# Two VectorE loops of flow attention written out, with the next tile's scaling ahead of the result

## What is computed

```
def _flow_attention(x, Wq, bq, Wk, bk, Wv, bv, Wo, bo):
    ...
    kv = jnp.einsum('nhld,nhlm->nhdm', k, v * source_competition[..., None])
    o = jnp.einsum('nhld,nhdm->nhlm', q * sink_incoming[..., None], kv)
    o = o * sink_allocation[..., None]
    o = o.transpose(0, 2, 1, 3).reshape(B, L, D)
    return o @ Wo + bo
...
sa = _flow_attention(_layernorm(x, g1, be1), Wq, bq, Wk, bk, Wv, bv, Wo, bo)[0]
x = x + sa
h = _layernorm(x, g2, be2)
h = jax.nn.gelu(h @ W1 + b1, approximate=False) @ W2 + b2
return x + h
```

## Time and profile before

| | us |
|---|---|
| median of 3 runs | 2020.53 |
| lowest and highest run | 2018.15, 2022.69 |
| the profiled execution, its own time | 2014.01 |
| its span, first to last instruction | 2012.2 |
| TensorE busy in the span | 1719.1 |
| VectorE busy | 911.8 |
| ScalarE busy | 535.0 |
| GpSimd busy | 747.8 |

### The profile page before, as it was taken

One profiled execution on the slowest core, in us unless ns is written; L12 is line 12 of the kernel. 1 busy time (PEld: TensorE's weight loads), 2 busy tenths in 40 slices (PEclk: granted clock), 3 DMA queues, 4 the chain that ended last, 5 costly groups with the idle time before them and its releaser, 6 DMA issues. The chain is left out here.

```text
span 2012.2 us, 26298 instructions
## 1 busy us (share of the span) xinstructions
PE 1719.1 (85%) x8051; PEld 1119.1 (56%) x8052; DVE 911.8 (45%) x2251; ACT 535.0 (27%) x1490; POOL 747.8 (37%) x857
## 2 busy tenths in 40 slices
PE   4559988756868888889689999599999999999996
PEld 4124433424447777754344445567776777677763
DVE  5852267343659999979756648300000000000001
ACT  0011111111148888821111115212211222112211
POOL 0577777773048988971011100300000000043007
PEclk9999989988979999999799999699999999999998
DMA  7800021000020000010210012864404400420003
GB/s 226 311 2 2 2 80 33 2 2 1 22 96 0 0 0 0 0 53 0 100 47 0 0 62 107 281 218 187 187 16 188 182 21 16 188 67 21 16 23 105
DMA packets 75240, 144.17 MB, mean 72 GB/s; under 512 B 20825, under 2 KB 22441, under 8 KB 70957
## 3 DMA queue, kind: packets, MB, share of 16 engines
q1 hardware_dynamic: 49201, 119.88, 16.3%
q0 software_dynamic: 18976, 10.95, 2.4%
q10 hardware_dynamic: 7006, 12.69, 1.9%
HBM read 107.75 MB, written 35.69 MB: 71 GB/s over the span
## 5 line engine op out<-in xcount | busy, mean ns | idle before, releaser
L326 POOL DMA_INDIRECT sorted_edges<-fa_records,fa_edge_slot x313 | 313.0, 1000 | 157.9 <-issue 100.4
L1926 PEld LDWEIGHTS et_ps_h<-ex_turned,arena 128*128 128x128 f32 x3072 | 349.3, 193 | 19.6 <-issue 19.6
L1926 PE MATMUL et_ps_h<-ex_turned,arena 128*128 128x128 f32 x3072 | 349.6, 276 | 8.5 <-issue 8.5
L1936 PE MATMUL et_ps_y<-arena,et_hidden_t 128*128 x768 | 337.5, 592 | 0.0
L1844 DVE TENSOR_SCALAR ex_turned<-et_ps_t,ex_ln_g,ex_ln_b 128x128 f32<-128x128 f32 x96 | 32.8, 403 | 580.4 <-PE et_ps_t L1906 580.4
L945 POOL TENSOR_SCALAR ad_row<-iota,ad_edges 128x128 fp32r<-128x128 f32 x295 | 210.6, 726 | 130.7 <-DMA ad_edges<-sorted_edges 101.1
L1936 PEld LDWEIGHTS et_ps_y<-arena,et_hidden_t 128*128 128x128 f32 x768 | 142.2, 190 | 160.7 <-issue 160.7
L994 ACT ACTIVATE ad_row_high<-ad_row,ad_edges 128x128 fp32r<-128x128 f32 x472 | 184.2, 391 | 46.2 <-DVE ad_row L965 33.0
L1016 PE MATMUL ad_ps<-ad_to,ad_row_high 128*128 128x320 f32 x472 | 153.4, 337 | 49.3 <-ACT ad_row_high L994 46.7
L1812 POOL DMA_INDIRECT xn_rows<-slot_out,from_slots x10 | 12.2, 1217 | 476.5 <-POOLq L1809 473.7
L963 DVE TENSOR_SCALAR ad_to<-iota,ad_edges 128x320 fp32r<-128x320 f32 x472 | 167.9, 415 | 20.6 <-DMA ad_edges<-sorted_edges 20.6
(11 more groups left out here) (381 smaller groups left out, 2219.8 us busy)
## 6 DMA issues: line engine op xcount, KB each, us to landing
arena<-L_ffn_W SPq DMA_DIRECT2D x16, 4096.0 KB, 18.5
slot_rows<-fa_zeros SPq DMA_DIRECT2D x1, 7424.0 KB, 26.9
slot_out<-fa_zeros SPq DMA_DIRECT2D x1, 7168.0 KB, 46.2
slot_out<-et_y ACTq DMA_DIRECT2D x24, 256.0 KB, 2.0
et_rows_in<-slot_rows ACTq DMA_DIRECT2D x24, 256.0 KB, 2.7
sorted_edges<-fa_records,fa_edge_slot POOLq DMA_INDIRECT x313, 2.1
arena<-x SPq DMA_DIRECT2D x1, 2500.0 KB
neighbour<-fa_Wv SPq DMA_DIRECT2D x10, 250.0 KB
```

Of the source, the lines that this page charges most:

```text
L326: nc.gpsimd.indirect_dma_start(g.sorted_edges, bass.IndirectOffsetOnAxis(ap=self.edge_slot[0:rows, e:e + 1], axis=0), self.records[0:rows, ...
L1926: last = pe.matmul(ps_h[:, f % 2, i, :], x.weights[:, at:at + P], turned[:, k, :], start=(k == 0), stop=(k == KD - 1))
L1936: last = pe.matmul(ps_y[:], hidden_t[:, i, :], x.weights[:, bass.ds(buffer * (2 * HALF) + (HALF + i * D), D)], start=(i == 0), stop=(i == ...
```

## The change

In both loops VectorE's call of `staggered` is replaced by ten tiles written out. `scale_q(t + 2)` now stands ahead of `attended(t)`, and `prepare_ff(t + 2)` ahead of `add_up(t)`. The orders of the other engines, the semaphores that are waited for and their values per tile, the buffers and the arithmetic are as they were.

```
-            staggered(c, 2, scale_q, attended, nothing)
+            scale_q(0, 0)
+            scale_q(1, 1)
+            for t in range(T):
+                if t + 2 < T:
+                    scale_q(t + 2, t % 2)
+                attended(t, t % 2)
...
-            staggered(c, 8, prepare_ff, nothing, add_up)
+            prepare_ff(0, 0)
+            prepare_ff(1, 1)
+            for t in range(T):
+                if t + 2 < T:
+                    prepare_ff(t + 2, t % 2)
+                add_up(t, t % 2)
```

## The result

The changed kernel took 2009.54 us, the median of four runs (2005.42 to 2010.44), against 2020.67 for the kernel before beside it (2018.15 to 2022.69). That is 11.1 us or 0.55% less by the medians; the ratio of the runs, as it was measured, is 0.9935 with a 95% interval of 0.9914 to 0.9956, which is 13.1 us. The forecast was 2006.0 in a range of 1999.5 to 2013.0, so the time lies in it and on the forecast side, 3.5 us above the value.

The account below looks back on a forecast made before the run. The prediction took the VectorE-TensorE chain through both loops as the bound. Savings of 13.8 us (attention) and 0.7 (feed-forward), 14.5 together, took the median from 2020.53 to 2006.0 us, range 1999.5 to 2013.

Parts of the forecast that it names:

- What bounds it: First block: VectorE and TensorE waiting for each other in turn form one chain through both loops, setting the block's end.
- Part 1: Attention loop: scaling and turn leave the chain, nine periods of 5.24 us, 47.2 against 60.96, 13.8 us less.
- open sizes: Attention loop: product 3.71 or 3.64 us, hand-over to TensorE up to 0.15 or 0.06; 1.1 us of the range.
- The clock's 5.0: Attention loop: three periods stretched by the lower clock return to normal, 5.0 us of the gain if the clock stays up.
- The Trainium skill's pull-ahead of weight loads: Attention loop: product's weight loads could slip under the turn, making 14.4 us instead of 13.8; the last tile spoke against it.
- Part 2: Feed-forward loop: order unchanged, hardware-loop register work goes, 0.12 us a tile over six tiles, 0.7 us less.
- the 14.5: Whole kernel: total predicted saving, 13.8 us from the attention loop plus 0.7 from the feed-forward loop.
- Part 4: After the loops: later stretches and next blocks shift as a whole, GpSimd's scatter stays hidden, block ends near 553.
- The clock did not fall in the attention loop: Rival: clock still falls in the attention loop, three times 1.67 us; saving 9.5, time 2011.0 us; chance 0.13.
- Swallowed: Rival: product waits for something else keeping its pace, or another engine ends the block; about 2020 us; chance 0.04.
- slower: Rival: clock stays at the lower level through the whole attention loop; 2038.4 us; chance 0.03.
- in step: Rival: all seven feed-forward periods fall to 7.79 us, 8.2 us more saved, 1997.8 us; chance 0.06.

Follow-up runs that it names:

- e5: Changed kernel with attention products going to two banks in turn; 2314.47 us, ratio 0.9893 to the kernel before.
- e4: Kernel before plus two unread products in TensorE's attention wait, tiles 0 to 7; 2011.45 us against 2015.67, ratio 0.9975.
- e3: Changed kernel plus three unread products in TensorE's feed-forward wait, tiles 0 to 6; 1993.48 us, ratio 0.9889 to the kernel before.
- e10: Kernel before with only the attention loop changed, plus three unread products in the feed-forward hardware loop's TensorE wait; 2320.29 us against 2344.11, ratio 0.9895.
- e2: Kernel before with only the feed-forward loop written out; 2020.57 us against 2015.67, ratio 1.0017.
- e11: Changed kernel run again, beside e12 on the same chip; 2335.15 us against 2344.11 for the kernel before, ratio 0.9967.
- e12: Kernel before with only the attention loop changed, same kernel as e1, run beside e11; 2328.59 us against 2344.11, ratio 0.9931.
- e1: Kernel before with only the attention loop changed, feed-forward hardware loop kept; 2003.57 us against 2015.67, ratio 0.9941.
- e8: e2 plus a 128-column clearing of a dead buffer between VectorE's last two steps of a tile; 2344.75 us against 2340.70, ratio 1.0018.
- e9: e2 plus a 192-column clearing of a dead buffer behind VectorE's last step, tiles 1 to 6; 2348.12 us against 2344.11, ratio 1.0014.
- e6: Changed kernel with prepare_ff(t + 3) instead of prepare_ff(t + 2) ahead of add_up(t); 2293.83 us, ratio 0.9801 to the kernel before.

## Why the prediction was right, point by point

- **What bounds it.** Right. The chain result, scaling, turn, product set the attention period; with the scaling ahead it is result and product, and two banks (e5) show that this was all that was left.
- **Part 1, 13.8 us.** Measured 13.5: nine periods of 5.27 us against 5.24. Of this, some 1.0 us is register work and not order (e4's rows); the sum had it in the 0.72 of L673 to L674. The last tile of before was the right row to take. Of the open sizes, the product stayed at the long end, 3.67 us behind its wait and 3.71 from its start to L673's, and the hand-over took 0.14. The clock's 5.0 is 4.9 by e4, and it was 1.00 throughout the new loop. Two sizes of the text were off without weight: TensorE stands still 1.17 us a tile, not 0.9, and ScalarE's copy starts 0.75 us after the turn starts (405.23 to 405.98 in the earlier trace rows), not 0.3; it is still done 0.48 us before the product of the tile before it (382.12 + 0.58 to 383.18).
- **The Trainium skill's pull-ahead of weight loads**, weighed in part 1: what the rows show is that the array stood free for 1.17 us and the product still took 3.67. The product's first loads, in the kernel before and in the changed one:

```profile
405.60 0.30 PEld L784 LDWEIGHTS fa_banks<-arena,fa_turned 128*125 128x125 f32 x2
...
383.15 0.29 PEld L794 LDWEIGHTS fa_banks<-arena,fa_turned 128*125 128x125 f32 x2 [1.37 <-ACT fa_turned L718]
```

  Before, they start under the turn, which runs from 405.23 to 405.88; now they start 0.11 us after L674 ends. By the Trainium skill, "TensorE: Matmul & The Clock Gate", section "Architectural detail: the array is 16× 32×32, not 1× 128×128", loads may go ahead of matmuls in flight. The trace of the kernel before agrees; in the changed loop none went ahead of a product still waiting for a semaphore, so the 14.4 did not come.
- **Part 2, 0.7 us.** Right as a mechanism, wrong as a result. The failed step is "I expect the same number" of slow periods. The register work is worth 0.77 us when the clock is held (e3 against e10). Without that the written-out loop lost 3.4 us (e2) and 6.6 (e11 against e12), while the first runs of the changed kernel and of e1 show no difference (0.9935 against 0.9941). Losses of this size take the 14.5 down to the 11.1 (by the medians) or 13.1 (by the ratio) that were measured. The range had two periods of 1.65 us for it, about the right size, but as an accident in either direction, where on the whole it is a loss. In the four profiles of the plain written-out loop with its 3.5 us wait (changed, e2, e5, e11) 10 of 28 full periods are over 10 us, in the two padded ones (e8, e9) 12 of 14, and in the four of the hardware loop (before, e1, e4, e12) 5 of 28. That the time stayed in the range is in part luck: with e11's loss instead of the 0.7 gained, the sum gives 2006.0 + 0.7 + 6.6 = 2013.3, just past the range's end.
- **Part 4.** Right: the untouched stretches moved as a whole, within 2 us. ScalarE's last copy came at 557.89 and not near 552.6, 5.3 us late, most of it (4.8) from the feed-forward loop.
- **Rivals.** The clock did not fall in the attention loop in any of the profiles with the new order. "Swallowed" and "slower" did not come. What came was the price of *in step* with its sign turned: I had asked only whether the feed-forward loop could get out of the slow rhythm, not whether it could fall into a slower one.
- **What stays open.** That a period's kind comes from the clock is shown (e3, e10). Why the written-out form meets the long kind more often is not: that its tile is 0.12 to 0.15 us shorter is the one difference in its rows, but the pads meant to restore it added 0.04 us at most. One form alone also has different rows of periods: the plain written-out loop had three long ones in the changed kernel, e2 and e11 and one in e5; the hardware loop had none (before, e12), two (e1) or three (e4), and e1 and e12 are the same kernel. So something outside the loop's own form counts as well, and ten profiles don't tell how much is the form's. A pad that VectorE must wait for wasn't tried.

## What to carry to other kernels

Where two engines take turns, write down both orders side by side and ask for each step whether the other engine's next step needs it: a step for a tile further on belongs ahead of the wait for the result, and one extra tile of lead (e6) or one extra bank (e5) can be worth more than anything in the steps. The same edit in two loops is not the same change: compare the order of instructions first, since in one of the two here nothing had moved. And do not count a saving of 0.1 us a tile in a loop in which TensorE stops for 3.5 us each tile; there the clock's rhythm is worth ten times that (1.7 to 2.6 us a period), and taking away the stop is the remedy.

## What the runs showed of the hardware that was not expected

- Work that nobody reads made the kernel faster: 2.7 us of unread products in a 3.5 us wait of TensorE's, in seven tiles, took 12.7 us off the feed-forward loop (72.99 to 60.28 in the profiles), and 1.9 us in a wait of 2.1 to 2.3 us took 4.9 off the attention loop.
- A loop and the clock can settle into a period that repeats to 0.01 us: 10.25 us, at a mean clock of 0.67, where the same work takes 7.63 at clock 1.00.
- Where the later eight kernels ran, the kernel before took 2341 to 2344 us instead of 2016 to 2021. The attention loop was the same to 0.1 us in either order (60.9 and 47.4 us); the difference lies ahead of them. A part of it is that from 114 to 176 us most of VectorE's register instructions took 0.7 us or more each. The statistics loop L211 by source line, first the kernel before in its first profile, then e12:

```profile
L211 DVEq FUSED_REGOPS  x25: 53/65/93, 106.7 to 440.4; - x25
```

```profile
L211 DVEq FUSED_REGOPS  x10: 700/1048/1397, 135.4 to 171.1; - x10
```

  The first loop of statistics (ten instructions of 0.69 us) ran from 106.8 to 112.9 us in the one and from 133.4 to 171.2 in the other, so this loop accounts for 32 of the 325 us. The largest part stands at L593, VectorE's additions to the next products: its thirty run from 126.3 to 255.4 us in the one and from 199.2 to 579.6 in the other, 251 us more, with 284 us of waits for which the profile shows no releaser. L593's own register instructions, 57 to 82 ns from 365.8 us on, are as fast there as before, and GpSimd still scatters at that time (to 472 us), so the scatter alone does not make them slow. What makes either slow was not tried. In those runs the two loops of this change start at 700 us, where VectorE's register instructions are fast again (36 to 99 ns in its loops after 480 us), so they say nothing of it.
- VectorE starts a short independent instruction under its neighbours, as the rows of e8 and e9 show: a clearing of 128 or 192 columns, 0.17 and 0.22 us long, moved the rest by nothing and by 0.04 us.
